# First layer's last step: VectorE makes the fourth tile of weights ahead of the elu, and the fifth ahead of the second layer's top

## The reference, cut to what matters

```python
# layer 0 and, with other weights, layer 2
Wh = x @ W;  s1 = Wh @ a1;  s2 = Wh @ a2
e = leaky_relu(s1[:, :, None] + s2[:, None, :], 0.2)
att = softmax(e + where(adj == 0, -1e9, 0), axis=2)
x = layernorm(x + elu(att @ Wh))
# layer 1
feat = softplus(x * (w0 / sqrt(2)) + b0)
scores = feat * wa + ba
logits = where(adj > 0, scores[:, None, :, :], -1e9)
x = layernorm(x + einsum('bijd,bjd->bid', softmax(logits, axis=2), feat))
# layer 3: dot-product attention with 4 heads, then one more such layer
```

## Time and profile before

| | us |
|---|---|
| median of 3 runs | 1974.04 |
| lowest and highest | 1972.91, 1974.85 |
| the profiled execution | 1975.19 |
| its span, first to last instruction | 1973.1 |
| TensorE's mean granted clock in it | 0.987 |

### The profile page before, as it was taken

The page is one execution under the profiler, slowest core; times in us unless marked ns, Lnnn a source line. Parts: engine busy times, 40 slices in busy tenths (PEclk is TensorE's granted clock), DMA queues, the critical chain, the costliest instruction groups (busy, mean ns, idle before and its releaser), DMA issues.

```text
span 1973.1 us, 51833 instructions
## 1 busy us (share of the span) xinstructions
PE 1888.3 (96%) x22292; PEld 1169.6 (59%) x22292; DVE 1632.1 (83%) x1944; ACT 1248.5 (63%) x2299; POOL 574.9 (29%) x440
## 2 busy tenths in 40 slices
PE   7999889999999899999999999999999999999994
PEld 6888767677888544554545545545455454554553
DVE  6999868878999777878888788888887888888875
ACT  3777776655877676566566665665656656656552
POOL 1233368862333200113122121231221312213124
PEclk9999999999999999999999999999999999999997
DMA  6000000000000001010110110101101011011011
GB/s 178 4 3 3 3 1 1 1 1 3 3 4 3 12 23 44 13 50 6 45 39 12 50 32 20 39 12 50 39 12 51 9 42 39 12 50 38 13 35 27
DMA packets 57068, 50.59 MB, mean 26 GB/s; under 512 B 36232, under 2 KB 39368, under 8 KB 56840
## 3 DMA queue, kind: packets, MB, share of 16 engines
q1 hardware_dynamic: 54936, 46.85, 9.1%
q10 hardware_dynamic: 1904, 0.43, 0.1%
HBM read 25.76 MB, written 4.72 MB: 15 GB/s over the span
## 4 chain that ended last, share of the span: by engine, by line
PE 64%; DVE 1%; DMA 0%; ACT 0%; issue 0%; POOL 0%; SPq 0%; ACTq 0%; DVEq 0%; POOLq 0%
PE fourth_ps_out L1689 24%; PE fourth_ps_scores L1639 9%; PE fourth_ps_out L1704 6%; PE fourth_ps_scores L1642 6%; PE fourth_ps_scores L1645 6%; PE fourth_ps_scores L1663 2%; PE fourth_ps_prep L1579 2%; PE fourth_ps_scores L1666 2%; PE fourth_ps_scores L1672 1%; PE fourth_ps_scores L1669 1%; PE fourth_ps_prep L1589 1%; PE fourth_ps_prep L1571 1%; PE fourth_ps_prep L1620 0%; PE fourth_ps_prep L1549 0%; PE fourth_ps_prep L1564 0%; PE fourth_ps_prep L1561 0%
## 5 line engine op out<-in xcount | busy, mean ns | idle before, releaser
L1234 DVE TENSOR_TENSOR fourth_weights<-fourth_weights,keep_mask 128x1024 f32<-128x1024 f32 x512 | 660.8, 1332 | 99.1 <-ACT fourth_weights L1480 96.2
L1480 ACT ACTIVATE fourth_weights<-fourth_ps_scores 128x1024 f32<-128x1024 f32 x512 | 496.9, 1024 | 333.9 <-PE fourth_ps_scores L1645 297.9
L1689 PE MATMUL fourth_ps_out<-fourth_weights,fourth_x_stage 128*64 128x512 f32 x2048 | 497.1, 605 | 0.3 <-DVE fourth_weights L1234 0.3
L615 DVE SCALAR_TENSOR_TENSOR additive_weights<-additive_ps_row,additive_gain,keep_mask 128x1024 f32<-128x1024 f32 x256 | 319.4, 1267 | 2.7 <-ACT additive_ps_row L730 2.7
L852 PE MATMUL additive_ps_out<-additive_values,additive_weights 128*64 128x65 f32 x8192 | 286.3, 227 | 30.9 <-DVE additive_weights L615 24.3
L852 PEld LDWEIGHTS additive_ps_out<-additive_values,additive_weights 128*64 128x64 f32 x8192 | 259.6, 140 | 56.0 <-DVE additive_weights L615 37.2
L1689 PEld LDWEIGHTS fourth_ps_out<-fourth_weights,fourth_x_stage 128*64 128x64 f32 x2048 | 124.2, 136 | 245.6 <-issue 215.6
L1639 PE MATMUL fourth_ps_scores<-fourth_g_high,fourth_x_high 64*128 64x512 f32 x1024 | 229.6, 445 | 2.1 <-ACT fourth_weights L1480 2.1
L1639 PEld LDWEIGHTS fourth_ps_scores<-fourth_g_high,fourth_x_high 64*128 64x128 f32 x1024 | 95.7, 183 | 201.0 <-ACT fourth_weights L1480 95.4
L1642 PE MATMUL fourth_ps_scores<-fourth_g_high,fourth_x_low 64*128 64x512 f32 x1024 | 202.2, 391 | 0.0
L1645 PE MATMUL fourth_ps_scores<-fourth_g_low,fourth_x_high 64*128 64x512 f32 x1024 | 200.7, 388 | 0.0
(11 more groups left out here) (243 smaller groups left out, 2741.0 us busy)
## 6 DMA issues: line engine op xcount, KB each, us to landing
fourth_recip_wide<-recip_out SPq DMA_DIRECT2D x128, 128.0 KB, 2.9
opening_adj<-in_adj SPq DMA_DIRECT2D x8, 512.0 KB, 8.0
fourth_x_high<-fourth_x_high SPq DMA_DIRECT2D x32, 128.0 KB, 2.4
fourth_x_low<-fourth_x_low SPq DMA_DIRECT2D x32, 128.0 KB, 2.3
fourth_h_high<-fourth_h_high SPq DMA_DIRECT2D x32, 128.0 KB, 2.7
fourth_h_low<-fourth_h_low SPq DMA_DIRECT2D x32, 128.0 KB, 2.4
out<-keep_x SPq DMA_DIRECT2D x15, 256.0 KB, 2.6
dens_out<-fourth_mixture SPq DMA_DIRECT2D x64, 4.0 KB
```

The source lines that it names most:

```text
L615: dve.scalar_tensor_tensor(out=weights[t % RING][:, :], in0=ps_row[s][:, :], scalar=gain[s][:, t:t + 1], in1=keep.mask[:, t, :].bitcast(F3 ...
L1234: dve.tensor_tensor(buf, buf, keep.mask[:, st.t, cols(half)].bitcast(F32).unsqueeze(1) .to_broadcast([P, 2, HALF]), ALU.mult).then_inc(wei ...
L1480: act.activation(weights[st.slot + half][:, :], ps_scores[half][:, :], ACT.Exp)\
L1689: last = pe.matmul(ps_out[rows(g), cols(half)], x_stage[st.s][:, st.t % PER_BANK, st.t // PER_BANK, :], weights[st.slot + half][:, cols(g) ...
```

## The change

In the last step of the first layer, and in no other, the weights of tile 3 are made ahead of `apply_elu` (they stood behind the second layer's `find_tile_top`), and those of tile 4 ahead of the second layer's `find_top` (they stood behind it). The other 31 steps of the two additive layers keep their order, and so do the other engines.

```diff
--- before.py
+++ after.py
@@ -636,6 +636,8 @@
         def step(b):
             n, s = first + b, b % 2
             ahead = b + 1 < BATCH
+
+            weights_first = first == 0 and not ahead
             weigh(n, s, 0)
             if b:
                 divide(n - 1)
@@ -649,14 +651,20 @@
                 norm.variance(dve, n - 1)
             if ahead:
                 find_minus_top(n + 1)
+            if weights_first:
+                weigh(n, s, 3)
             if b:
                 apply_elu(n - 1)
             if ahead:
                 find_top(n + 1)
             beside.vector(b, 2)
-            weigh(n, s, 3)
-            beside.vector(b, 3)
-            weigh(n, s, 4)
+            if weights_first:
+                weigh(n, s, 4)
+                beside.vector(b, 3)
+            else:
+                weigh(n, s, 3)
+                beside.vector(b, 3)
+                weigh(n, s, 4)
             if ahead:
                 copy_tops(n + 1)
             beside.vector(b, 4)
```

## The result

The changed kernel takes 1971.17 us (median of 10 runs, 1968.43 to 1974.05), the kernel before 1975.05 in the same comparison (10 runs, 1972.91 to 1977.79): 3.88 us less, a ratio of 0.9982 with a 95% interval of 0.9974 to 0.9991, so 1.8 to 5.1 us. The profiled execution took 1969.32 us, its span 1967.2.

A forecast was written before the change was run, and what follows sets the result against it. A chain over several engines, with VectorE and TensorE waiting in turn, sets the pace there. VectorE's idle 1.16 + 2.43 + 0.49 = 4.08 us caps the gain; 1974.04 - 4.1 = 1969.9 us, range 1968.0 to 1972.6.

The forecast's parts named there:

- Before the elu: First layer's last step: the elu now waits for GpSimd's product, so find_tile_top starts 0.04 us later.
- later pair: A later GpSimd product (1.30 us) and two-input VectorE operation (1.34 us, ending 0.29 behind it), used to size the elu.
- Rival E: The elu gets in only behind GpSimd's product and the 1.64 us rstd: gain 2.4 us, 1971.6; chance 0.03.
- In front of find_top: find_top starts without a wait at 236.01 instead of 238.49, 2.48 us earlier, with one STT already done.
- To the shift: Second layer's shift comes at 239.93 against 244.05, 4.1 us earlier at TensorE's full clock, or 3.8.
- Behind the shift: Head of the second layer follows rigidly, first matmul at about 245.0; nothing fixed in time can catch the gain.
- Rival D: The gain is taken back in the second layer, whose engines wait for each other: 1974.0 us; chance 0.08.
- The clock: Term left open: TensorE's low clock costs 1.0 us before the shift and 1.5 us at the second layer's head.
- Rival B: The median run doesn't pay the 1.0 us of low clock before the turn: gain 3.1 us, 1970.9; chance 0.17.
- A: The forecast itself: gain 4.1 us, 1969.9 us; chance 0.55.
- Rival C: TensorE keeps full clock through the second layer's head too, 1.5 us more gain: 1968.4 us; chance 0.12.
- F: Full clock not earned back until late in second layer's second step, 26 us more low clock: +8.9 us, 1982.9; chance 0.05.

The follow-up runs named there:

- second comparison: The changed kernel again against the kernel before on one chip, 11 runs against 31: ratio 0.9981 (0.9972 to 0.9990).
- tile 3 alone: Against the kernel before, only tile 3's weights go ahead of the elu, tile 4's stay behind find_top: 1970.26 us against 1973.72, ratio 0.9980.
- tile 4 alone: Against the kernel before, only tile 4's weights go ahead of find_top, tile 3's stay behind find_tile_top: 1973.1 us against 1973.72, ratio 1.0000.

## Why the prediction was right, step by step

**Before the elu.** The product took 1.29 us (1.30 taken), the elu 0.78 and ended 0.55 behind the product's end (0.53 taken, though the prediction doesn't show how this follows from the 0.29 of its later pair); find_tile_top started 2.93 us after the variance's start against 2.87 before: +0.06 for +0.04. That the order of the conflict turns round was right. Not foreseen was that the elu in its turn delays rstd, 2.10 us for 1.64. GpSimd's queue had the room: the residual ended at 235.87, the reduction began at 236.60, so the 0.8 us that I gave this cover were 0.7. Rival E, the elu behind rstd as well, is out by the elu's 0.78 us.

**In front of find_top.** No wait, as worked out: 5.07 us after the variance's start instead of 7.51, 2.44 earlier (2.48 forecast). The sum takes 1.05 us for a tile as a third of 3.02, which is 1.01, and then adds 1.15; the tile took 1.15, and there was room for either. The two experiments with one tile each show that my account of this wait was the right one: it hung on TensorE's order, tile 3 ahead of the turn, not on VectorE's load.

**To the shift.** Variance to shift 8.98 us; forecast 239.93 - 230.98 = 8.95, with TensorE at full clock, which it had. The gain of 4.09 and the 4.10 at the first matmul are the forecast sum.

**Behind the shift.** The chain of engines followed rigidly, as said: 4.10 us at the first matmul in both profiles. Behind it that holds in the first profile alone, as far as the third layer's last divide (4.08); in the second 2.9 us are left there. "Nothing fixed in time can catch the gain" was right for engines and DMA, but the clock took a part: 1.2 us at the second layer's head in one of two profiles and 0.8 us in the third layer in both. Rival D, a gain taken back whole by the waits of the second layer, is out.

**The clock.** Rival B put 1.0 us of the gain down to luck of one execution. Both profiles of the kernel before show the same 1.93 us of tile 3. The gain of 3.1 us that it left was too high besides: tiles 4 and 5 took 3.33 us for two in the kernel before, against 2.30 at full clock, so without the low stretch the 0.49 us wait for the spread top would have gone as well, and B's gain would have been about 2.6 us (an estimate from these times). In time terms it can't be told apart from A: 3.9 us of difference of medians, interval 1.8 to 5.1. Rival C (the low clock at the second layer's head goes too) didn't come: 2.68 and 3.78 us for the eight matmuls, and 3.24, 3.78, 3.78 and 3.78 in the four other profiles that keep this order of shift and tiles 6 and 7. My ground against it, that the 1.98 us of idle stay, held as far as seen; only versions in which a low stretch came earlier, upon tiles 6 and 7, got 2.11 us. So the cost that the prediction kept was kept, and in five of these six profiles it was larger than the 3.16 us before. F, with 26 us more of low clock, fell: from 262 to 400 us the granted clock was 1.00 in all twelve profiles. But its direction, more low clock behind the change, was right for 0.8 us in the first profile and 2.0 in the second.

**Where the last tenths are.** What the runs add to the sum is the clock in other places. The third layer's last step has its own gap, 3.96 us in which TensorE waits for tile 3. In both profiles of the kernel before the low clock came just behind this tile (1.20 and 1.25 us), in both of the change upon it (2.00):

```profile
655.10 1.20 PE L852 MATMUL additive_ps_out<-additive_values,additive_weights 128*64 128x65 f32 x32 [3.96 <-DVE additive_weights L615]
```

```profile
649.88 2.00 PE L860 MATMUL additive_ps_out<-additive_values,additive_weights 128*64 128x65 f32 x32 [3.96 <-DVE additive_weights L615]
```

VectorE's first product for the fourth layer waits for matmuls queued behind this tile, 1.68 us before and now 2.49:

```profile
653.50 1.22 DVE L1204 TENSOR_TENSOR fourth_products<-fourth_ps_prep,fourth_x_high 128x1024 fp32r<-128x1024 f32 x1 [2.49 <-PE fourth_ps_prep L1572]
```

That is the 0.8 us given back in the last column. It isn't the luck of one execution: all five other profiles that change the first layer's last step and leave the third layer's alone show the 2.00 us too. Why the low clock falls otherwise there, in a step whose instructions and 3.96 us gap are the same, is not shown.

The clock shows over the runs too. Of 57 runs of the kernel before that were made beside the experiments, the 11 with a mean granted clock of 0.985 took 1975.4 us on average, the 17 with 0.988 took 1972.2. Of the change's first ten, the four at 0.986 took 1973.2, the four at 0.989 1969.0. That is as much as the change is worth, so the chances of 0.49 and 0.44 on both sides of 3.95 us were a fair account of a local gain of 4.1. That the medians said 3.88 is in part luck. The traces carry 3.3 and 2.1 us to the fourth layer's first scores, from there to the end the twelve profiles take between 1304.8 and 1308.5 us, and the second comparison's medians are 3.1 us apart.

## What to carry to other kernels

When two engines wait in turn for each other, look at what stands in each one's queue behind the wait, and whether some of it is already allowed. An operation whose inputs and buffer are free should stand in front of a wait, not behind it; the more so if its reader has the next link of the chain queued behind it (tile 3 alone, 3.5 us at the next layer's first matmul), and less if it only fills the wait (tile 4 alone, 1.6 us). The joints between stages are the places to look: the same kind of edit with three tiles at another joint gave nearly 4 us more (ratio 0.9962 against 0.9981). And where TensorE must have a gap, try to put it where a slow matmul behind it has cover; the events bear this out here (second batch's shift at 22.89 against 24.70 and 25.88), the times alone don't. Last, a gain read at one event isn't yet a gain at the end: follow it through the later stages, in more than one profile.

## What was not expected of the hardware

- GpSimd's power over 8 columns (rstd, 1.65 us) didn't hold up a VectorE operation with two inputs that began in the midst of it (0.68 us), but took 2.10 and 2.02 us where it began under such an operation. The Trainium skill, SBUF — State Buffer, section "Who interferes with whom", has the shared pair of ports as an exclusive lock, held for the whole instruction by whoever issues first, and a VectorE instruction with two SBUF inputs contending for it with a GpSimd instruction that reads SBUF. The 128 x 512 product agrees (the elu took 0.78 us); rstd, in the order rstd first, does not (0.68 us, in one profile).
- The single runs of this one-core kernel lie up to 8 us apart (1970.5 to 1978.5), and 3 to 4 us of it go with TensorE's mean granted clock, with the same instructions. Where two profiles of one kernel were compared, what differed was which matmuls behind a gap got 1.2 GHz. In the orders with the shift ahead of tiles 6 and 7 it fell on these two tiles in all four profiles (3.30 to 3.54 us for two), and the head of the second layer had 2.11, 2.11, 2.11 and 2.41 us for its eight matmuls. Whether that is due to the earlier low stretch or to the shorter wait at the head itself (0.92, 0.95, 0.22 and none) the runs don't separate.
